# Setup of a fused convolution kernel: the order in which tables, the first image, the row weights and the constants are transferred

## The reference, cut to what matters

```python
x = x + _L0_conv_ref(_gn(x), L0_conv_w, L0_conv_b)                      # 1x1 mixing, leaky ReLU, min-max scaling
x = x + _L1_conv_ref(_gn(x), L1_conv_w_real, L1_conv_w_imag, ...)        # 3x3 convolution of the spectrum
x = x + _L2_conv_ref(_gn(x), L2_conv_weight_int8, ...)                   # 3x3, quantized input
x = x + _L3_conv_ref(_gn(x), L3_conv_weight)                             # 3x3, circular
```

## Time and profile before

| | us |
|---|---|
| median of three runs | 6607.25 (6604.26 to 6617.34) |
| the profiled execution, its time | 6610.31 |
| its span | 6608.5 |
| TensorE's first matmul | 259.93 |
| last minimum of the first mixing ends | 338.4 |
| first instruction behind the barrier | 350.61 |

### The profile page before, as it was taken

The page is one execution under the profiler, slowest core; times in us unless marked ns, Lnnn a source line. Parts: engine busy times, 40 slices in busy tenths (PEclk is TensorE's granted clock), DMA queues, the critical chain, the costliest instruction groups (busy, mean ns, idle before and its releaser), DMA issues. The chain is left out here.

```text
span 6608.5 us, 201426 instructions
## 1 busy us (share of the span) xinstructions
PE 5692.0 (86%) x64138; PEld 3660.6 (55%) x64138; DVE 4927.7 (75%) x9721; ACT 4543.5 (69%) x8808; POOL 2744.1 (42%) x4633
## 2 busy tenths in 40 slices
PE   0279979979989989988988988994989889889889
PEld 0048748848757757856766865771434334334334
DVE  2977877887887887887887877887667667667664
ACT  1767767767776766767766546556877878778776
POOL 1256556555555556546646546550111111111112
PEclk9989989989999999999999999997999999999999
DMA  5416615625634633643642541552767667667665
GB/s 178 164 34 188 185 53 177 187 71 160 185 95 138 185 117 117 185 138 95 185 154 59 142 137 43 142 142 45 192 168 199 167 171 202 165 164 201 168 170 137
DMA packets 535622, 959.18 MB, mean 145 GB/s; under 512 B 121947, under 2 KB 126683, under 8 KB 532827
## 3 DMA queue, kind: packets, MB, share of 16 engines
q1 hardware_dynamic: 467546, 799.21, 43.8%
q10 hardware_dynamic: 67456, 151.01, 6.9%
HBM read 560.66 MB, written 287.60 MB: 128 GB/s over the span
## 5 line engine op out<-in xcount | busy, mean ns | idle before, releaser
L1610 PE MATMUL pC<-xs,taps 128*128 128x512 f16 x4608 | 1093.3, 382 | 109.1 <-DMA xhalo<-xs 100.2
L963 PE MATMUL pM<-gw,xh 64*128 64x256 f16 (+1 forms) x24960 | 1126.5, 244 | 0.0
L963 PEld LDWEIGHTS pM<-gw,xh 64*128 64x128 f16 x24960 | 967.9, 95 | 126.1 <-issue 2.9
L725 POOL TENSOR_TENSOR X<-X,zo 128x256 f32 (+1 forms) x512 | 371.2, 725 | 1245.6 <-DVE X L1074 1245.6
L1610 PEld LDWEIGHTS pC<-xs,taps 128*128 128x128 f16 x4608 | 448.3, 98 | 672.2 <-DVE xs L1659 89.7
L1506 POOL TENSOR_TENSOR xn<-xn,one_col 128x1 f32<-128x1 f32 x520 | 176.6, 340 | 1391.7 <-ACT xn L1540 1391.7
L1526 ACT ACTIVATE scaled<-X,qbias,qscale 128x512 f32 (+1 forms) x512 | 411.0, 804 | 353.5 <-DMA X<-after_layer 295.0
L272 PE MATMUL pM<-X,mix0s 64*64 64x512 f32 x2304 | 529.6, 635 | 131.9 <-DVE X L1046 108.3
L1548 ACT ACTIVATE xs<-xn 128x1028 f16<-128x1028 f32 x520 | 545.7, 1049 | 88.3 <-POOL xn L1507 87.5
L1074 DVE SCALAR_TENSOR_TENSOR X<-pZ,X 128x512 f32 (+1 forms) x512 | 353.9, 691 | 328.4 <-ACT zo L784 327.2
L710 POOL TENSOR_TENSOR X<-X,rl 128x512 f32 x384 | 477.9, 1274 | 269.5 <-ACT rl L755 269.4
(11 more groups left out here) (241 smaller groups left out, 13775.8 us busy)
## 6 DMA issues: line engine op xcount, KB each, us to landing
gw<-row_weights SPq DMA_DIRECT2D x520, 288.0 KB, 3.2
after_layer<-X SPq DMA_DIRECT2D x512, 256.0 KB
out_dram<-result SPq DMA_DIRECT2D x512, 256.0 KB
X<-in_x_dram SPq DMA_DIRECT2D x448, 256.0 KB
X<-after_layer ACTq DMA_DIRECT2D x224, 512.0 KB, 5.8
stage<-in_x_dram SPq DMA_DIRECT2D x192, 512.0 KB
xhalo<-xs SPq DMA_DIRECT2D x504, 96.4 KB, 3.6
qhalo<-q SPq DMA_DIRECT2D x496, 96.2 KB, 4.0
```

The costliest lines, as they stand in the source:

```text
L725: nc.gpsimd.tensor_tensor(X[:, j, 0], X[:, j, 0], zo[:, k], ALU.add)
L963: nc.tensor.matmul(pY[:, r, col:col + nd * P], row(xh, r)[:, k, p, ri, off:off + P], weights(r, q_, d, nd, ri), start=ri == 0 and off == 1 ...
L1610: nc.tensor.matmul(bank, taps3[:, d, wh], xs[:, h, own, d:d + W], start=d == 0 and n == 0, stop=False)
```

## The change

SP still issues the tables first, but then goes straight to the stores, in a loop that is written out. Behind the store of pair 1 it issues the four small constants, and behind each store from pair 2 to pair 18 one of the seventeen of `loads`. ScalarE waits for the tables before it issues anything; then come chunks 0 to 2, and behind the spread of pair n, for even n up to 24, chunk 3 + n/2. The first four pieces of image 1 are issued behind the spreads of pairs 28 to 31. ScalarE's loop is written out too. Nothing that is computed changes.

```diff
-                        repeated(mix0c, w0, setup_in)
-                        for dst, src in ((bre, b1r), (bim, b1i)):
-                            sp.dma_start(whole(dst), src.rearrange("(c a) -> c a", a=1).unsqueeze(0).broadcast_to([BANDS, C, 1])).then_inc(setup_in, 16)
-                        sp.dma_start(whole(bias0), b0.rearrange("(a n) -> a n", a=1).broadcast_to([P, 1])).then_inc(setup_in, 16)
-                        for dst, src in loads:
-                            sp.dma_start(whole(dst), src).then_inc(setup_in, 16)
-
                         pairs = gscr[1:J + 1].rearrange("(n t) p w -> n p t w", t=2)
-                        with sp.Fori(0, J // 4) as g:
-                            for k in range(2):
-                                sp.wait_ge(hi_ready, g * 2 + k + 1)
-                                sp.wait_ge(lo_ready, g * 2 + k + 1)
-                                sp.dma_start(pairs[g * 2 + k], gbuf[:, k]).then_inc(stored[k], 16)
+                        for n in range(PAIRS):
+                            sp.wait_ge(hi_ready, n + 1)
+                            sp.wait_ge(lo_ready, n + 1)
+                            sp.dma_start(pairs[n], gbuf[:, n % 2]).then_inc(stored[n % 2], 16)
+                            if n == 1:
+                                repeated(mix0c, w0, setup_in)
+                                for dst, src in ((bre, b1r), (bim, b1i)):
+                                    sp.dma_start(whole(dst), src.rearrange("(c a) -> c a", a=1).unsqueeze(0).broadcast_to([BANDS, C, 1])).then_inc(setup_in, 16)
+                                sp.dma_start(whole(bias0), b0.rearrange("(a n) -> a n", a=1).broadcast_to([P, 1])).then_inc(setup_in, 16)
+                            if 2 <= n < 2 + len(loads):
+                                dst, src = loads[n - 2]
+                                sp.dma_start(whole(dst), src).then_inc(setup_in, 16)
...
-                        for c in range(J // 4):
+                        def chunk(c):
                             act.dma_start(Xf[:, 4 * c:4 * c + 4], image_view(0)[:, :, 4 * c:4 * c + 4]).then_inc(image_in[c], 16)
...
-                        for p in range(4):
-                            stream(p)
                         act.wait_ge(tables_in, n_tables)
-                        with act.Fori(0, J // 4) as g:
-                            for k in range(2):
-                                act.wait_ge(comp_ready, g * 2 + k + 1)
-
-                                act.wait_ge(stored[k], (g + 1) * 16)
-                                for s in range(HB):
-                                    m = spread_hi(k, s)
-                                m.then_inc(hi_ready, 1)
+                        for c in range(3):
+                            chunk(c)
+                        for n in range(PAIRS):
+                            act.wait_ge(comp_ready, n + 1)
+
+                            act.wait_ge(stored[n % 2], (n // 2 + 1) * 16)
+                            for s in range(HB):
+                                m = spread_hi(n % 2, s)
+                            m.then_inc(hi_ready, 1)
+                            if n % 2 == 0 and 3 + n // 2 < J // 4:
+                                chunk(3 + n // 2)
+                            elif n >= PAIRS - 4:
+                                stream(n - PAIRS + 4)
```

## The result

| | before | after |
|---|---|---|
| median of six runs each, us | 6611.97 (6604.26 to 6620.91) | 6580.36 (6572.86 to 6595.73) |
| the profiled execution, its time | 6610.31 | 6585.46 |
| its span | 6608.5 | 6583.6 |
| TensorE's first matmul | 259.93 | 233.33 |
| first instruction behind the barrier | 350.61 | 324.44 |

The ratio of the times is 0.9955, with a 95% interval of 0.9942 to 0.9968: 21 to 38 us faster. The forecast was 60 us; the sign held, the size was half. The median lies near the upper end of the range, where the rival "chunks stay slow" (6579) had been put.

The account below looks back on a forecast made before the run. The setup before TensorE's first matmul (259.93 us) bounds the kernel. Pair 6 at 54, plus 104, 21.7, sumw 9 and tail 11.25, gives 200, 60 us earlier: 6550.3, or 6547.2 against the median; forecast 6530 to 6565, range 6515 to 6585.

Parts of the forecast that it names:

- chunks stay slow: Rival for the pair loop: chunks keep the early rate, 6.8 us per pair over 20 pairs, 6579 to 6588; chance 0.15.
- What bounds the kernel, and what moves with it: Setup before PE's first matmul at 259.93 us: moving that point moves the end by as much; 60 us earlier.
- Tables: Start of the setup: small tables land at about 7 to 8 us, not 30.34; first comph ready at 14.
- The start behind three chunks: First pairs: early stores queue behind chunks at 8.2 us each; pair 6 ready at 54, costing 17 us (0 to 23).
- The loop of two halves: Steady pairs: spreading pair n+2 waits until store n has landed, and an even store lands with the chunk, 8.0 us.
- The size of that wait: Pairs 7 to 26: chunk 5.0 us, even pairs 10.4 us apart, 5.2 per pair, 104 us for 20 pairs.
- the bound of 13.6: Upper bound for two pairs with chunks at the early rate: 8.2 + 1.65 + 1.3 + 2.4 = 13.6 us.
- What decides is latency, not bytes: Pair loop: the bytes fit, with 8.3 us of work in 8.68 on the chunk-carrying half; two gbuf halves make landing decide.
- sumw: 2 MB constant behind pair 18's store: the next stores queue behind it, 9 us once, between 0 and 12.
- The last five pairs: End of the pair loop: five pairs at 4.34 us each, 21.7 us.
- The tail: After the last comph: twelve moments and the aggregate, 11.25 us until PE starts.
- Everything is hidden: Rival: stores pass a chunk in little more than 2.9 us, start costs nothing; PE at 157 to 175, 6503 to 6522; chance 0.15.

Follow-up runs that it names:

- e3: Changed kernel with chunks 3 to 15 issued only behind the last pair (moments incomplete); no total time compared, mv ready at 162.7 us.
- e8: Changed kernel with three gbuf slots in place of two; 6573.61 us, PE's start at 217.9.
- e13: Changed kernel with every chunk, at the same place, issued as two transfers of two tiles (4 KB rows); 6546.55 us beside 6613.34 for the kernel before.
- e2: Changed kernel with chunks 3 to 15 issued two at a time behind every fourth pair; 6588.21 us, PE's start at 229.2.
- e7: Changed kernel with chunks issued by SP, each as eight transfers, one per band; 6525.40 us beside 6614.59 for the kernel before.
- e1: Changed kernel reduced to tables first: all sixteen chunks and four image-1 pieces issued at once, constants ahead of stores; 6640.66 us beside 6596.88 for the kernel before.
- e6: Changed kernel with whole chunks issued by SP in the stores' queue, each behind an even store; 6551.76 us, PE's start at 200.5.
- e4: Changed kernel with all 21 constants issued behind the last store; 6608.24 us beside 6596.88 for the kernel before.

## Why the prediction was right in kind and wrong in size

- **What bounds the kernel, and what moves with it**: right. PE's start moved by 26.6, the barrier by 26.2, the span by 24.9. The image-1 sums stayed hidden.
- **Tables**: in at 5.32, not 7 to 8; the first `comph` was ready at 11.47 (forecast 14). This gain was lost in the next step, which ended 2.3 us late.
- **The start behind three chunks**: store 2 landed at 51.4 (forecast 48, at most 53), pair 6 was ready at 56.3 (forecast 54). Right; it was priced with the early rate.
- **The loop of two halves**: who waits for whom is as told. ScalarE waits for the even store, which waits for the chunk; `e3` takes the chunks away and the wait goes.
- **The size of that wait**: this step failed. "I take 5.2, since chunks after 56 ran at the full rate" put 5.0 us on a chunk; in the loop it takes 8.8 by the share of its queue. The rounds are 13.1 us and not 10.4, near the bound of 13.6 that stood beside it. From pair 6 to pair 26 the trace has 137.5 us (56.3 to 193.8) against 104 + 9: 24.5 of the 33.4 missing. The wrong price also overturned the sentence "What decides is latency, not bytes": the half of the engines that carries chunks has 8.8 + 3.3 = 12.1 us of work in a round, not 8.3 in 8.68, and `e8` shows that a third slot doesn't make up for that. One term was missing on the other side: the chunk is issued 2.2 us before the store (51.55 and 53.76), so 8.8 + 1.65 + 1.3 + 2.4 = 14.2 is 1.1 too much.
- **Where the 5.0 came from**: the row from 96 to 108 us was one of a queue that had read without a break for 50 us, with 0.23 of 2.51 MB beside it. The kernel before had a nearer row. From 84 to 88 us `sumw` was in flight beside a chunk, and the chunks' queue moved 0.45 MB at a share of 48.9%: 9.1 us a chunk, where it was 5.1 from 72 to 84.
- **What `e13` says of it**: with rows of 4 KB the same plan starts PE at 199.3, so the size of the wait is in good part in how the transfer is cut. That this is the forecast's 200 is partly luck, since its start was earlier (46.4, not 54) and its rounds longer (11.5, not 10.4) than the sum had them.
- **`sumw`**: four pairs around it (143.08 to 173.78) took 30.7 us where two rounds take 26.2, so it cost about 4.5, not 9. The overestimate hid part of the miss above.
- **The last five pairs**: 28.3 us, not 21.7. The last chunk is issued behind pair 24, and pairs 25 and 26 are spread only from 199.74 on, when the stores beside it have landed (in the order of time above). The sum ended the loop one round early: 6.6 us.
- **The tail**: 11.25 us, as forecast.

The misses are 2.3 + 24.5 + 6.6 = 33.4 us, which is 233.3 less 200. Of the rivals, "chunks stay slow" (PE at 232) is what happened, for which I had named a reason (a chunk into an empty queue) that `e2` does not bear out. "Everything is hidden" fell with landings of 10.7 us. The rule of the Trainium skill on the outermost dimension ("DMA: Bandwidth & Descriptors", section "Why a DMA increments its semaphore by 16 and not by 1"), which I had used only to explain the share of 0.51, turned out to be the way to a better kernel: in `e7` the share is 1.03.

**Open.** Why rows of 8 KB are slow in one stretch and fast in another. They were slow from the start to about 50 us in the kernel before, to about 88 in `e1`, for the whole loop in the changed kernel, and less so in the stores' own queue (`e6`). A large transfer beside them goes with it (84 to 88 us in the kernel before), but from 8 to 48 us, where it was as slow, there were only 0.49 MB beside 4.95. Rows of 4 KB and one shared queue each take a part of the slowness away; whether both act on the same thing is not known.

## What to carry to other kernels

Price a transfer by the row in which it runs as the change will have it run (alone or beside others, first or in a long series), and where two rows differ as 8.2 and 5.0 us do, let the forecast rest on the nearer one instead of the quieter one. A mean share of 0.67 does not say that the DMA engines have room: where a transfer uses half of them, count its queue on that half. Where a loop waits for a small number of buffers, ask first whether those engines are full, since a further buffer hides latency and not work (a third slot gave 15 us here, chunks by band in SP's queue gave 60). Before moving a large transfer, look at how it is cut: its share of the DMA engines (0.51 here) and the length of its rows decided more (233 to 199, and to 173) than where it was put.

## What the hardware showed that was not expected

- From 8 to 48 us of the kernel before, an image read in rows of 8 KB went with all else at 136 GB/s, in rows of 4 KB at 208. Of the 2.9 MB gained, 2.1 were those of the other queue, and the tables landed at 14.6 instead of 30.3.
- Once a chunk on half of the engines was over, the stores behind it moved at a share of 0.53, as if only half of the engines had anything left to do.
- A third buffer slot lengthened the stores' landing from 10.7 to 17.4 us and gave back 15 us in all.
- Twenty-one constants, when they stood behind the last store, cost VectorE 44.9 us of waiting (`e4`); between the stores they made a round 0.7 us longer.
- Tables first, and nothing else, made PE's start 17 us later.
